# A gated delta-rule attention between two feed-forward layers: key taps ahead of the gates, squares beside the chunks, and the value passes of the next unit spread over four steps

## The chip, the cores and the metric

One Trainium2 chip, one core of it. The metric is the time of one execution on the device in microseconds (us); lower is better. All times below are in us unless ns is written.

## The reference

`x` is 4 sequences of 512 tokens, 512 wide. The output is three residual layers in a row: half a feed-forward layer (2048 wide, its weights spline-interpolated from few control points), a gated delta-rule attention, and half a feed-forward layer again. The change touches the attention alone. Cut to what matters:

```python
q, k, v, z = split(layernorm(x) @ W_qkvz)          # 16 key heads, 32 value heads, 128 wide
q, k, v = silu(causal_conv4(q, k, v))              # four taps along the tokens
q, k = rms_norm(q) / 128, rms_norm(k) / sqrt(128)
for t in range(512):                               # per value head, state 128 x 128
    S = S * exp(g[t])
    delta = (v[t] - k[t] @ S) * beta[t]
    S = S + outer(k[t], delta)
    out[t] = q[t] @ S
y = (silu(z) * rms_norm(out) * norm_w) @ W_out
```

## The kernel before

The attention runs over 64 units, one key head (2 value heads, `R` = 2) of one sequence (512 tokens, 4 chunks of 128, `CH` = 4); four units in a row share a head's weights. The recurrence is done in chunks: per chunk and value head a triangular matrix is inverted, and then a state of 128 x 128 goes from chunk to chunk.

The work is a pipeline with an order written out by hand. Slot `j` of the loop does three things: the delta work of unit `j` (`has_delta`), the preparation of unit `j+1` (`has_prep`: projections, convolution, norms, decays, the matrix to invert), and the output of unit `j-1` (`behind`: scaling, turning and projecting the gated heads). Each engine has its own pass (`pe_pass` L1677, `act_pass` L2005, `dve_pass` L2189, `pool_pass` L2388), runs in order, and waits on counters of the other engines through `wait(engine, name, value)` (L1571 on). The names' first letter tells who counts: s TensorE, a ScalarE, d VectorE, p GpSimd, l loads.

A slot has two parts. The first is steps 2 to 13 (L1882): six levels of the triangular inverse, for the two heads in turn (`g = s % 2`). In each step TensorE makes a product into `psP` (4 matmuls), does what the list `fill[s]` holds, and then the update of the inverse (8 matmuls, L1905 and L1907), for which VectorE must have masked the product (L2336). The product of step s needs ScalarE's copy (`copy_t`, L2090) of the update of step s-2. Then come `residual` (L1912), `fill[14]`, the second residual and `newton` (L1923), `fill[15]`, the second Newton step and the turn of the scaled keys (`turn_kn`, L1784). A residual is followed by VectorE's correction (L2344) that its Newton step needs; ScalarE copies the first inverse out (`inverse_out`, L2140), scales the keys (`scale_k`, L2064, with GpSimd's factor `p_rk`, L2487 to L2491), and then copies the second inverse.

The second part is the loop over the four chunks. TensorE turns the values, subtracts the state's part, makes deltas and outputs and updates the state; between these stand the twelve lists `gap`, with more projections and the decays of the next unit. At the end TensorE projects the next queries (nine passes), ScalarE squares the outputs of both heads (`squares`, L2101, 4 chunks each, an ACTIVATE and a read of the accumulator per chunk), and VectorE multiplies the outputs by the gates (L2378).

What fills the steps:
- Projections of the next unit in passes of 512 columns (`proj_part`, L1702), 12 per unit of keys K, queries Q and two values V0 and V1; gates Z0 and Z1 of this unit in passes of 256 columns (`gate_part`, L1724), 24 each. They use two PSUM banks: K, V0, Z0 the one, Q, V1, Z1 the other. A bank is free when its reader has ended (`bank_free`); for V0 that is the gates' product on VectorE (`silu_z`, L2220, L2223).
- `turn_gated` (L1739, four turns in L1747) of a head that GpSimd has scaled (`scale_gated`, L2438, L2441, behind `out_scale`, L2428, which makes the factor from the squares); ScalarE and VectorE split it in a high and a low half (`gated` L2110, `low` L2243); `out_product` (L1750, six matmuls of 512 columns), of which each of four is added by VectorE (`out_add`, L2248, L2253).
- `turn_k` (L1773, L1781) of the next keys, which ScalarE then squares (`square_k`, L2055, L2061). It overwrites `kn`, which GpSimd's `ks` product (L2469) reads, and so waits for `p_ks`.
- On ScalarE the first tap of a convolution (`tap`, L2015), on VectorE the other three (`conv`, L2204, L2209); the tanh of the silus and gates on ScalarE (`tanh` L2025, `tanh_z` L2038), the silus of K, Q and V1 on GpSimd (`silu`, L2443: L2447 and L2448), in that queue's order: scaling of the heads, V1, K, `kg`, `nllo`, `ks`, Q, the key factor. In the third unit of each head but the last, GpSimd splits half a weight part (L2405 to L2412) between Q and the key factor.
- `qk` (L2225, L2228) on VectorE reads the product of keys and queries from PSUM bank `psM`, into which the next turn goes.

PSUM: `psO[0]` is the upper half of `psT[1]` and `psO[1]` is `psP`, so the outputs of a unit stand where the next unit's level 0 (`level_0`, L1816, head 1 in `fill[2]`) and step products go.

## Time and profile before

| | |
|---|---|
| median of 3 runs | 3610.79 (3608.39 to 3610.88) |
| the profiled execution's own time | 3609.92 |
| its span | 3608.0 |
| TensorE matmul busy | 3391.7, 94% of the span |
| VectorE, ScalarE, GpSimd busy | 2282.5, 2090.2, 2268.8 |
| mean granted TensorE clock | 0.983 of full |

Before the attention stand the splines and the first feed-forward layer (to about 430), behind it the second (from about 3320). A timeline row has start, duration, engine, line, operation, and in brackets the idle time before it with what ended it; an engine's records overlap where it is pipelined, so for TensorE the distance between two starts tells more than the idle time. `PEld` is the weight load of a matmul, SP is the queue of the transfers.

### The profile page before, as it was taken

The page shows a single profiled execution, that of the slowest core. Times are in us where ns is not written, and L with a number is a line of the kernel's source. Part 1 is how long each engine was busy: PE and PEld are TensorE (multiplying, and loading weights), DVE is VectorE, ACT ScalarE, POOL GpSimd, SP SyncE. Part 2 cuts the span into 40 slices and gives each one's busy share as a digit, 9 for nine tenths or more (in the row PEclk, how much of TensorE's full clock was granted, in tenths as well). Part 3 has the DMA queues.
Part 4 walks back from the last instruction along what each step waited for, and adds up shares of the span by engine and source line. Part 5 has one row for each costly group of instructions (what it writes and reads, how often), then busy time and mean ns, then how long its engine had stood idle before and what let it go on. Part 6 is the DMA issues. An engine that isn't in the chain of part 4 may idle for free. (4 is left out here: it accounts for less than half of the span.)

```text
span 3608.0 us, 77463 instructions
## 1 busy us (share of the span) xinstructions
PE 3391.7 (94%) x29092; PEld 2441.0 (68%) x29092; DVE 2282.5 (63%) x4402; ACT 2090.2 (58%) x5699; POOL 2268.8 (63%) x2680
## 2 busy tenths in 40 slices
PE   5997699999999999999999999999999999995998
PEld 3886366666666666666666666666666666663787
DVE  4654566666666666666666666666666666663564
ACT  3443566666666666666666666666666666662343
POOL 2111677777777777777777777777777777772010
PEclk8998899999999999999999999999999999997999
DMA  3524112222222222222222212222222221112421
GB/s 139 180 48 78 49 65 71 76 74 73 78 69 79 75 72 78 68 76 73 76 74 73 79 68 79 68 79 68 79 67 81 66 80 66 59 60 76 141 48 36
DMA packets 217313, 274.46 MB, mean 76 GB/s; under 512 B 91248, under 2 KB 127344, under 8 KB 215792
## 3 DMA queue, kind: packets, MB, share of 16 engines
q1 hardware_dynamic: 207680, 253.60, 22.7%
q0 software_dynamic: 4464, 14.36, 1.1%
q8 instruction: 234, 3.83, 0.5%
q10 hardware_dynamic: 4800, 1.56, 0.3%
q14 instruction: 135, 1.11, 0.1%
HBM read 180.12 MB, written 89.16 MB: 75 GB/s over the span
## 5 line engine op out<-in xcount | busy, mean ns | idle before, releaser
L2099 ACT ACTIVATE at_t<-at_inv 128x512 f16<-128x512 f32 x768 | 460.8, 600 | 434.6 <-PE at_inv L1907 434.4
L2336 DVE TENSOR_TENSOR at_pml<-at_prod,at_cst 128x256 f16<-128x256 f32 x768 | 323.1, 421 | 212.5 <-PE at_prod L1681 201.8
L2483 POOL TENSOR_TENSOR at_gm<-at_cst,at_gates 128x512 fp32r<-128x512 f32 x256 | 268.3, 1069 | 230.3 <-PE at_misc L1681 230.3
L1681 PE MATMUL at_proj<-x_hi,at_w_hi 128*128 128x512 f16 x1024 | 389.3, 380 | 2.8 <-PEq L1267 2.8
L1681 PE MATMUL at_proj<-x_lo,at_w_hi 128*128 128x512 f16 x1024 | 389.8, 381 | 0.0
L1681 PE MATMUL at_proj<-x_hi,at_w_lo 128*128 128x512 f16 x1024 | 389.1, 380 | 0.0
L1905 PEld LDWEIGHTS at_inv<-at_pml,at_t 128*128 128x128 f16 x3072 | 226.4, 97 | 119.0 <-DVE at_pml L2336 81.0
L1681 PE MATMUL at_prod<-at_t,at_nlhi 128*128 128x64 f16 (+1 forms) x3584 | 287.0, 196 | 19.4 <-DVE at_cv_z L2378 15.7
L2209 DVE SCALAR_TENSOR_TENSOR at_cv_v<-at_proj,at_cw,at_cv_v 128x511 f32<-128x511 f32 (+2 forms) x384 | 287.5, 749 | 21.8 <-ACT at_cv_v L2023 8.3
L2253 DVE SCALAR_TENSOR_TENSOR rows<-at_misc,first_tab,rows 128x512 f32<-128x512 f32 x256 | 191.1, 746 | 168.1 <-PE at_misc L1681 168.1
L1905 PE MATMUL at_inv<-at_pml,at_t 128*128 128x64 f16 x3072 | 285.8, 193 | 11.9 <-DVE at_pml L2336 1.1
L1907 PE MATMUL at_inv<-at_t,at_pml 128*128 128x64 f16 x3072 | 283.5, 193 | 0.0
L1681 PE MATMUL at_proj<-at_w_hi,x_hi 128*128 128x256 f16 x1024 | 279.5, 273 | 1.6 <-DVE at_cv_q L2209 0.9
L1681 PE MATMUL at_proj<-at_w_lo,x_hi 128*128 128x256 f16 x1024 | 279.0, 272 | 0.0
L1681 PE MATMUL at_proj<-at_w_hi,x_lo 128*128 128x256 f16 x1024 | 278.9, 272 | 0.0
L1037 PE MATMUL f_ring<-f_x_hi,ffn_w 128*128 128x512 f32 x640 | 247.6, 402 | 3.3 <-DVE f_x_lo L929 2.9
L2165 ACT ACTIVATE at_t<-at_inv,at_gates 128x128 f32<-128x128 f32 x512 | 159.5, 363 | 155.4 <-PE at_inv L1681 155.4
L1681 PEld LDWEIGHTS at_prod<-at_t,at_nlhi 128*128 128x128 f16 x3584 | 190.4, 97 | 82.5 <-issue 45.0
L1907 PEld LDWEIGHTS at_inv<-at_t,at_pml 128*128 128x128 f16 x3072 | 210.3, 98 | 39.2
L1681 PE MATMUL at_misc<-at_wo_hi,at_gt_hi 128*128 128x512 f16 x512 | 198.4, 388 | 22.8 <-DVE at_gt_lo L2246 16.3
L2358 DVE SCALAR_TENSOR_TENSOR at_t<-at_t,at_dcy,at_inv 128x128 f32<-128x128 f32 x256 | 77.6, 345 | 195.9 <-PE at_inv L1681 188.9
L1681 PE MATMUL at_misc<-at_wo_hi,at_gt_lo 128*128 128x512 f16 x512 | 196.1, 383 | 0.0
(323 smaller groups left out, 10124.3 us busy)
## 6 DMA issues: line engine op xcount, KB each, us to landing
rows<-x SPq DMA_DIRECT2D x64, 1024.0 KB, 5.5
x<-rows SPq DMA_DIRECT2D x64, 1024.0 KB, 4.3
at_gb<-decays SPq DMA_DIRECT2D x64, 512.0 KB, 3.7
at_raw_w<-w_qkvz SPq DMA_DIRECT2D x48, 512.0 KB, 7.5
ffn_weights<-ffn_w SPq DMA_DIRECT2D x1, 11776.0 KB, 35.5
ffn_w<-ffn_weights POOLq DMA_DIRECT2D x4, 2688.0 KB, 23.9
at_raw_o<-w_out SPq DMA_DIRECT2D x16, 512.0 KB, 3.5
f_xnext<-x_in SPq DMA_DIRECT2D x4, 1024.0 KB, 5.3
```

The costliest lines, as they stand in the source:

```text
L1037: return nc.tensor.matmul(out, lhsT, rhs, start=start, stop=stop)
L1681: return nc.tensor.matmul(out, lhsT, rhs, start=start, stop=stop)
L1905: nc.tensor.matmul(half_of(ch(psT[g], c), level, 0), ch(t16[:, g, 1], c), half_of(ch(pml[:, level - 1, g], c), level, 0), start=False, sto ...
L1907: last = nc.tensor.matmul(half_of(ch(psT[g], CH + c), level, 1), ch(pml[:, level - 1, g], c), half_of(ch(t16[:, g, 1], c), level, 1), star ...
L2099: own["a_t"].up(A(grown(t16[:, s % R].rearrange("p a t -> p (a t)"), s // R), grown(psT[s % R], s // R), ACT.Copy))
L2165: own["a_d"].up(A(delta[:, h, :], ch(psY, h), ACT.Copy, scale=gcur[:, 2, at + c, h:h + 1]))
L2209: ins = V.scalar_tensor_tensor(out[:, s:S], unit_bank[u][:, 0:S - s], cw[(j + 1) // B % 2][:, u, 3 - s:4 - s], out[:, s:S], ALU.mult, ALU.add)
L2253: own["d_y"].up(V.scalar_tensor_tensor(row, out_bank[:], tab[:, of // B % 2, 7:8], row, ALU.mult, ALU.add))
L2336: own["d_p"].up(V.tensor_tensor(pml[:, level - 1, g].rearrange("p (c b a m) -> p c b a m", c=CH, a=2, m=m)[:, :, :, 0, :], psP[:, 0:S // 2 ...
L2358: ins = V.scalar_tensor_tensor(state[:, h, :], state[:, h, :], dcy[:, j % 2, h, c:c + 1], ch(psU, h), ALU.mult, ALU.add)
L2483: last = G.tensor_tensor(gm[:, k], incl.unsqueeze(1).to_broadcast([P, CH, P]), new_gates[:, g, at:at + CH, h:h + 1].to_broadcast([P, CH, P ...
```

## The change

It moves work between places of the written order, and splits one task.
- `squares` is done per chunk: those of chunks 0 to 2 stand in the chunk loop of ScalarE, behind the deltas (and the second value's tap and first high copy in chunk 2, ahead of the query squares in chunk 1); those of the last chunk at the end, head 1 first. `s_o` counts every chunk and `a_sqo` five per unit (`SQ`). TensorE waits for the squares of chunk c-1 before it writes outputs of chunk c.
- VectorE does all three key taps at the end ahead of the gates (they were one in the chunk loop, one behind the gates, one in step 2), gates head 1 first, and does the first `qk` at the end and the second in step 2 (both were in step 3). TensorE's first product waits for the first gate alone, level 0 and the second head's for both.
- ScalarE: query tap in step 2 (was 4), the gated heads in 2 and 4 (3 and 5), tanh of V1 in 5 (2), of Z0 in 8 (9), key squares in 11 (12). VectorE: `low` in 4 and 6 (5 and 6), first query tap in 5 (6), the fourth `out_add` in 10 (11), the first gates' product in 10 (12).
- TensorE: the gated heads are turned in steps 3 and 5 (4 and 6); Z0 in parts of 4, 6, 4, 6, 4 passes in steps 3 to 7 (5, 5, 5, 2, 7); Z1 in 8 to 13 as 5, 5, 4, 4, 4, 2 (5, 5, 4, 4, 2, 4); the keys turned in 11 (12); V0 in 12 to 15 as 2, 3, 3, 4 passes (14 and 15 as 4, 8).
- GpSimd adds the constant of the norm to `qe` at the end of the preparation (`p_qe`) and not to `sso` behind the squares.

The diff, cut; lines are those of before and after, indentation shortened:

```diff
--- before.py
+++ after.py
@@ -1194,6 +1194,7 @@
 Q_EPS = 64 * D * D * EPS_RMS
+SQ = CH - 1 + R
@@ -1550,11 +1551,11 @@
...
@@ -1819,7 +1820,7 @@
             else:
-                wait(pe, "a_sqo", R * i)
+                wait(pe, "a_sqo", SQ * i)
                 wait(pe, "d_gate", R * i)
@@ -1839,29 +1840,28 @@
         if has_delta:
-            fill[3].append(gates_in(Z0_U, 0, 5))
-            fill[4].append(gates_in(Z0_U, 5, 10))
-            fill[5].append(gates_in(Z0_U, 10, 15))
-        if behind:
-            for h in range(R):
-                fill[4 + 2 * h].append(lambda h=h: turn_gated(h, j - 1))
-        if has_delta:
-            fill[6].append(gates_in(Z0_U, 15, 17))
-            fill[7].append(gates_in(Z0_U, 17, 24))
+            fill[3].append(gates_in(Z0_U, 0, 4))
+            fill[4].append(gates_in(Z0_U, 4, 10))
+            fill[5].append(gates_in(Z0_U, 10, 14))
+            fill[6].append(gates_in(Z0_U, 14, 20))
+            fill[7].append(gates_in(Z0_U, 20, 24))
             fill[8].append(gates_in(Z1_U, 0, 5))
...
             fill[10].append(gates_in(Z1_U, 10, 14))
+            fill[11].append(gates_in(Z1_U, 14, 18))
+            fill[12].append(gates_in(Z1_U, 18, 22))
+            fill[13].append(gates_in(Z1_U, 22, 24))
         if behind:
+            for h in range(R):
+                fill[3 + 2 * h].append(lambda h=h: turn_gated(h, j - 1))
             for c in range(WPROD):
                 fill[7 + c].append(lambda c=c: out_product(c, j - 1))
-        if has_delta:
-            fill[11].append(gates_in(Z1_U, 14, 18))
-            fill[12].append(gates_in(Z1_U, 18, 20))
-            fill[13].append(gates_in(Z1_U, 20, 24))
         if has_prep:
-            fill[12].append(turn_k)
-            fill[14].append(parts(V0_U, 0, 4))
-            fill[15].append(parts(V0_U, 4, 12))
+            fill[11].append(turn_k)
+            fill[12].append(parts(V0_U, 0, 2))
+            fill[13].append(parts(V0_U, 2, 5))
+            fill[14].append(parts(V0_U, 5, 8))
+            fill[15].append(parts(V0_U, 8, 12))
             gap[0].append(parts(V1_U, 0, 3))
@@ -1885,8 +1885,8 @@
                     wait(pe, "a_hi", R * j + g + 1)
-                    wait(pe, "a_sqo", R * j - 1 + g)
-                    wait(pe, "d_gate", R * j)
+                    wait(pe, "a_sqo", SQ * j)
+                    wait(pe, "d_gate", R * j - 1 + g)
                 if s == 2 * R - 1:
@@ -1963,6 +1963,7 @@
                     wait(pe, "p_qg", R * j + R)
+                    wait(pe, "a_sqo", SQ * j + c)
                     for h in range(R):
@@ -1985,9 +1986,8 @@
                     last = mm(ch(psO[h], c), ch(aqk[:, h], c), delta[:, h, :], c == 0, True)
-                if c == CH - 1:
-                    own["s_o"].up(last)
-                else:
+                own["s_o"].up(last)
+                if c < CH - 1:
                     turn_v(c + 1)
@@ -2019,7 +2019,7 @@
             if u == V0_U:
-                wait(act, "s_o", j)
+                wait(act, "s_o", CH * j)
             own["a_tap"].up(A(conv_out(u), unit_bank[u][:], ACT.Copy, scale=cw[(j + 1) // B % 2][:, u, 3:4]))
@@ -2098,13 +2098,15 @@
-        def squares(h):
-            wait(act, "s_o", j + 1)
-            wait(act, "p_fr", j)
-            if h < R - 1:
-                wait(act, "d_gate", R * j + h + 1)
-            for c in range(CH):
-                last = A(osq[:, h, c * P:(c + 1) * P], ch(psO[h], c), ACT.Square, scale=2 * D ** -0.5, accum_out=sso[:, h, c:c + 1])
+        def squares(c, h):
+            if c == 0:
+                wait(act, "p_fr", j)
+            wait(act, "s_o", CH * j + c + 1)
+            return A(osq[:, h, c * P:(c + 1) * P], ch(psO[h], c), ACT.Square, scale=2 * D ** -0.5, accum_out=sso[:, h, c:c + 1])
+
+        def squares_of(c):
+            for h in range(R):
+                last = squares(c, h)
             own["a_sqo"].up(last)
@@ -2115,20 +2117,21 @@
             steps[2].append(lambda: tap(K_U))
-        if has_delta:
-            steps[2].append(lambda: tanh(V1_U, j - 1))
+        if has_prep:
+            steps[2].append(lambda: tap(Q_U))
         if behind:
             for h in range(R):
-                steps[3 + 2 * h].append(lambda h=h: gated(j - 1, h))
+                steps[2 + 2 * h].append(lambda h=h: gated(j - 1, h))
+        if has_delta:
+            steps[5].append(lambda: tanh(V1_U, j - 1))
         if has_prep:
-            steps[4].append(lambda: tap(Q_U))
             steps[6].append(lambda: tanh(K_U))
...
         if has_delta:
-            steps[9].append(lambda: tanh_z(Z0_U))
+            steps[8].append(lambda: tanh_z(Z0_U))
         if has_prep:
-            steps[12].append(square_k)
+            steps[11].append(square_k)
         if has_delta:
@@ -2169,16 +2172,21 @@
                     tanh(V0_U)
+                if c == 2:
+                    tap(V1_U)
+                    high(j + 1, 0)
+            if has_delta and c < CH - 1:
+                squares_of(c)
+            if has_prep:
+                if c == 1:
                     square_q()
                 if c == 2:
-                    tap(V1_U)
-                    for g in range(R):
-                        high(j + 1, g)
+                    high(j + 1, 1)
         if has_prep:
...
             for h in reversed(range(R)):
-                squares(h)
+                own["a_sqo"].up(squares(CH - 1, h))
         if has_prep:
@@ -2222,9 +2230,9 @@
-        def qk(h):
-            wait(dve, "s_kq", j + 1)
-            wait(dve, "a_sqo", R * j)
+        def qk(i, h):
+            wait(dve, "s_kq", i + 1)
+            wait(dve, "a_sqo", SQ * i)
             own["d_aqk"].up(V.scalar_tensor_tensor(aqk[:, h, :], psM[:], -1.0, e2[:, h, :], ALU.mult, ALU.mult))
@@ -2305,26 +2313,21 @@
         steps = {s: [] for s in range(STEPS)}
-        if has_prep and has_delta:
-            steps[2].append(lambda: conv(K_U, (3,)))
         if has_delta:
-            for h in range(R):
-                steps[3].append(lambda h=h: qk(h))
+            steps[2].append(lambda: qk(j, 1))
         if has_prep and not has_delta:
...
         if behind:
-            steps[5].append(lambda: low(0, j - 1))
+            for h in range(R):
+                steps[4 + 2 * h].append(lambda h=h: low(h, j - 1))
         if has_prep:
-            steps[6].append(lambda: conv(Q_U, (1,)))
-        if behind:
-            steps[6].append(lambda: low(1, j - 1))
-        if has_prep:
+            steps[5].append(lambda: conv(Q_U, (1,)))
             steps[7].append(lambda: conv(Q_U, (2, 3)))
...
             for c in range(WPROD):
-                steps[7 + c + c // (WPROD - 1)].append(lambda c=c: out_add(c, j - 1))
+                steps[7 + c].append(lambda c=c: out_add(c, j - 1))
         if has_delta:
-            steps[12].append(lambda: silu_z(Z0_U))
+            steps[10].append(lambda: silu_z(Z0_U))
         for s in range(R, STEPS):
@@ -2369,15 +2372,15 @@
                     conv(K_U, (1,), j + 1)
+        if has_prep and j + 2 < UNITS:
+            conv(K_U, (2, 3), j + 1)
         if has_delta:
-            for h in range(R):
-                if h == 0:
-                    wait(dve, "s_o", j + 1)
-                else:
-                    wait(dve, "a_sqo", R * j + h)
+            for h in reversed(range(R)):
+                wait(dve, "s_o", CH * (j + 1))
+                wait(dve, "a_sqo", SQ * (j + 1) - h)
                 own["d_gate"].up(V.tensor_tensor(gated_of(h), psO[h].rearrange("p (c v) -> p c v", c=CH), gated_of(h), ALU.mult))
-        if has_prep and j + 2 < UNITS:
-            conv(K_U, (2,), j + 1)
+        if has_prep:
+            qk(j + 1, 0)
         if ends:
@@ -2427,17 +2430,16 @@
-            wait(pool, "a_sqo", R * (of + 1))
-            wait(pool, "a_sq", of)
+            wait(pool, "a_sqo", SQ * (of + 1))
+            wait(pool, "p_qe", of + 1)
             flat = sso[:].rearrange("p h c -> p (h c)")
             chain(G.tensor_tensor(sso[:], sso[:], qe[:, of % 2, :].unsqueeze(1).to_broadcast([P, R, CH]), ALU.add))
-            chain(G.tensor_scalar(flat, flat, Q_EPS * EPS_RMS, None, ALU.add))
             own["p_fr"].up(G.tensor_tensor(fr[:].rearrange("p h c -> p (h c)"), flat, half[:, 0:R * CH], ALU.pow))
...
-            wait(pool, "d_gate", R * of + h + 1)
+            wait(pool, "d_gate", R * (of + 1) - h)
             own["p_gt"].up(G.tensor_tensor(gated_of(h), gated_of(h), fr[:, h, :].unsqueeze(2).to_broadcast([P, CH, D]), ALU.mult))
@@ -2448,7 +2450,7 @@
         if has_delta:
-            wait(pool, "s_o", j)
+            wait(pool, "s_o", CH * j)
             wait(pool, "a_knT", j)
@@ -2510,6 +2512,8 @@
                 own["p_t0"].up(G.affine_select(right, right, [[0, CH], [-2, P // 2]], ALU.not_equal, 1.0, base=-1, channel_multiplier=1))
+            wait(pool, "a_sq", j + 1)
+            own["p_qe"].up(G.tensor_scalar(qe[:, nxt, :], qe[:, nxt, :], Q_EPS * EPS_RMS, None, ALU.add))
             if j == 0:
```

## Rows read from the trace of the kernel before

**Rows 1.** the page: span, and busy time of the engines
```profile
span 3608.0 us, 77463 instructions
...
PE 3391.7 (94%) x29092; PEld 2441.0 (68%) x29092; DVE 2282.5 (63%) x4402; ACT 2090.2 (58%) x5699; POOL 2268.8 (63%) x2680
```

**Rows 2.** windows, columns: stretch, its length, busy us and instructions of each engine, clock, DMA
```profile
480.00:3200.00 2720.00, 2653.74 (x25127) 1883.43 (x25128) 1806.64 (x3529) 1727.25 (x4970) 2038.87 (x2335) 1.00 0.23 73
3294.00:3318.00 24.00, 13.16 (x32) 4.37 (x32) 4.39 (x6) 1.19 (x2) 3.60 (x3) 0.50 0.03 12
```

**Rows 3.** waits of TensorE's weight loads, 1000 to 3000 us: total, times, longest
```profile
PEld at_inv L1905 <- DVE at_pml L2336: 54.3, 178, 0.4
```

**Rows 4.** timeline of TensorE, one unit: start, length, engine, line, operation, count, idle before
```profile
1509.53 0.66 PE L1747 MATMUL at_misc<-at_cst,at_cv_z 128*128 128x128 f32 x4 [0.33 <-POOL at_cv_z L2441]
...
1515.78 0.27 PE L1681 MATMUL at_proj<-at_w_hi,x_hi 128*128 128x256 f16 x1
...
1523.32 0.20 PE L1905 MATMUL at_inv<-at_pml,at_t 128*128 128x64 f16 x1
...
1525.80 0.22 PE L1681 MATMUL at_prod<-at_t,at_nlhi 128*128 128x128 f16 x1
...
1527.29 0.22 PE L1681 MATMUL at_prod<-at_t,at_nlhi 128*128 128x128 f16 x1
...
1529.90 0.61 PE L1787 MATMUL at_misc<-at_cst,at_kn 128*128 128x128 f32 x4
```

**Rows 5.** timeline of ScalarE, end of the unit: first and last of 16 square instructions
```profile
1548.42 0.28 ACT L2107 ACTIVATE at_aqk<-at_prod 128x128 f32<-128x128 f32 x1 [0.16 <-PE at_prod L1681]
...
1550.34 0.25 ACT L2107 ACTIVATION_READ_ACCUMULATOR at_aqk<-at_inv 128x1 f32 x1
```

**Rows 6.** timeline of VectorE, end of the unit
```profile
1546.86 0.75 DVE L2209 SCALAR_TENSOR_TENSOR at_cv_k<-at_proj,at_cw,at_cv_k 128x511 f32<-128x511 f32 x1 [0.61 <-ACT at_cv_k L2023]
...
1549.59 0.69 DVE L2378 TENSOR_TENSOR at_cv_z<-at_prod,at_cv_z 128x512 f32<-128x512 f32 x1 [0.41 <-ACT at_aqk L2107]
```

**Rows 7.** timeline of TensorE, end of the unit
```profile
1549.94 0.38 PE L1681 MATMUL at_proj<-x_hi,at_w_lo 128*128 128x512 f16 x1
...
1550.54 0.28 PE L1681 MATMUL at_prod<-at_t,at_nlhi 128*128 128x64 f16 x4 [0.22 <-DVE at_cv_z L2378]
1550.69 0.38 PE L1681 MATMUL at_inv<-at_pm,at_cst 128*128 128x512 f16 x1
```

**Rows 8.** timeline of GpSimd, the same unit
```profile
1506.07 0.20 POOL L2433 TENSOR_TENSOR at_sso<-at_sso,at_qe 128x8 f32<-128x8 f32 x1 [2.88 <-ACT at_aqk L2107]
...
1506.36 0.25 POOL L2434 TENSOR_SCALAR at_sso<-at_sso 128x8 f32<-128x8 f32 x1
...
1508.43 2.04 POOL L2441 TENSOR_TENSOR at_cv_z<-at_cv_z,at_fr 128x512 f32<-128x512 f32 x2
...
1514.15 1.27 POOL L2447 TENSOR_TENSOR at_th<-at_th,at_cv_k 128x512 f32<-128x512 f32 x1 [1.08 <-ACT at_th L2036]
...
1520.87 1.61 POOL L2469 TENSOR_TENSOR at_ks<-at_kn,at_gates 128x384 f32<-128x384 f32 x2
```

**Rows 9.** timeline of VectorE, steps 11 and 12
```profile
1523.17 0.74 DVE L2253 SCALAR_TENSOR_TENSOR rows<-at_misc,first_tab,rows 128x512 f32<-128x512 f32 x1
...
1524.22 0.68 DVE L2223 SCALAR_TENSOR_TENSOR at_cv_z<-at_th,at_proj 128x512 f32<-128x512 f32 x1
```

**Rows 10.** timeline of ScalarE, behind step 15
```profile
1528.65 1.13 ACT L2068 ACTIVATE at_kn<-at_misc,at_scale 128x128 f32<-128x128 f32 x4
```

**Rows 11.** timelines of GpSimd, ScalarE and TensorE, third unit of a head
```profile
1618.19 0.20 POOL L2491 TENSOR_TENSOR at_scale<-at_rr,at_cst 128x4 f32<-128x4 f32 x1
...
1618.42 1.14 ACT L2068 ACTIVATE at_kn<-at_misc,at_scale 128x128 f32<-128x128 f32 x4
...
1619.62 0.66 PE L1787 MATMUL at_misc<-at_cst,at_kn 128*128 128x128 f32 x4
```

**Rows 12.** timeline of TensorE, end of the last unit
```profile
3296.73 1.12 PE L1747 MATMUL at_misc<-at_cst,at_cv_z 128*128 128x128 f32 x4 [5.75 <-POOL at_cv_z L2441]
```

More of the change, by code:

```diff
@@ L1552, in attn_phase @@
                  "d_conv", "d_silu", "d_z", "d_nl", "d_aqk", "d_p", "d_e", "d_s", "d_gate", "d_lo", "d_y", "d_max_w", "d_max_o", "d_tab", "d_scaled", "d_scaled_o", "d_link",
[L1553 removed]
+                 "p_w", "p_wo", "p_z", "p_gt", "p_silu", "p_gm", "p_ex", "p_diag", "p_t0", "p_lo", "p_dcy", "p_kg", "p_qg", "p_ks", "p_rk", "p_fr", "p_qe", "p_link"]
         sems = {n: sem(n) for n in names}
[L1557 removed]
+        AHEAD = {"s_proj": 4, "s_qtr": 1, "s_ktr": 2, "s_dg": R,  "a_tap": 4, "a_th": 4, "a_ssk": 1, "a_sq": 1, "a_kn": 1, "a_knT": 1, "a_ex": R,
                  "d_conv": 4, "d_silu": 1, "p_silu": 3, "p_gm": R, "p_ex": R, "l_x": -32, "l_kq": -16, "l_v": -16, "l_z": -16, "l_wo": -16, "l_taps": -48, "p_w": -2, "p_z": -1, "p_rk": 1}
```

2 lines of the change are left out of this document (removed).

## The prediction

> **What bounds the kernel now.** I read the page first: of the span of 3608.0 us TensorE is busy 94%, the next engine 63% [rows 1]. The table of windows puts 2720 us of it, the 61 middle turns of the attention loop, at full granted clock, 2.4 GHz [rows 2]. So the attention is a TensorE stream with holes, and what an edit can win is a hole. The list of TensorE's waits names many small ones, the largest sum being the updates of a step behind VectorE's masked product, 54.3 in 2000 us [rows 3]. The timelines of one unit, which repeats every 44.75 us, then give each hole its place. I quote times of one unit; its first step product started at 1505.79, and that of the next unit starts at 1550.54. Matmul records overlap, so a hole is read from start to start: a pass of 256 columns follows another in 0.11, one of 512 in 0.22, and so the first gated head's turn at 1509.53 stands behind a hole of 0.50, of which its row shows 0.33 [rows 4].
>
> **The tail of a unit.** ScalarE squares the outputs in 16 instructions, from 1548.42 to 1550.59, 0.25 per chunk and head [rows 5]. The change leaves two of the eight, so the last ends at about 1549.05; the other six go into the chunk loop, a pair of 0.5 behind each chunk's outputs. There ScalarE waits for TensorE, so I cost them at nothing; without that cover each pair costs 0.5. The wait of chunk c+1 for these squares is over 0.2 to 0.6 before TensorE gets there. VectorE now runs all three key taps before the gates. They start at 1546.86, 0.75 each and one behind the other's end, so the gates, 0.61 apart, end at about 1549.78 and 1550.39, where the second ended at 1550.28 before [rows 6]. The first product no longer waits for the second gate and goes when the pass that starts at 1549.94 lets it, 1550.16; but level 0 of head 1, right behind it, does wait, and comes about 0.17 after the gate's end. That is 1550.55, where it stood 0.15 behind the product of 1550.54, at 1550.69: gain 0.15 [rows 7].
>
> **Steps 2 to 7.** GpSimd's scaling began with the squares' end: sum 1506.07, constant 1506.36, power, scaling 1508.43 [rows 8]. Squares 1.54 earlier and the constant (0.33 to the next start) taken out bring the scaling to 1506.55 and its first head to 1507.6. The turn, moved to step 3, is due at 1507.72: its hole of 0.50 closes. With fills of four and six passes, and a turn beside each four, the holes behind the mask's products close too, but ScalarE's longer queue (query taps and first gated head ahead of the copy of step 3) opens two of 0.15 at steps 5 and 7. Summed, Z1's first pass goes at 1514.39 and not at 1515.78 [rows 4]: 1.39 ahead. Steps 8 to 10 are as before and keep it.
>
> **Steps 10 to 13.** VectorE's fourth output sum (0.75) moves ahead of the mask of step 11, and the first gates' product (0.68) with it. In the old clock the sum was ready to start about 1522.49 but ran at 1523.17, then the gates at 1524.22 [rows 9]. Now: sum at 1521.10, gates 1521.76, mask of step 11 not before 1522.37 to 1522.79, updates of step 11 at 1522.82. They stood at 1523.32 [rows 4]; with the key turn (0.45) ahead of them I expect some 0.6 of holes in this step, and only 0.5 left of the 1.39. Steps 12 and 13 have fills of 0.87, longer than the 0.68 that a product's way through VectorE takes, so their holes close. They hold five of the values' twelve passes, 1.08 of work. The residual of head 0 starts at about 1525.5, against 1525.80 [rows 4].
>
> **Steps 14 and 15 give no more.** From there the time is a chain, not a stream: residual 1525.80, its correction by VectorE, second residual 1527.29 (1.49 later), Newton step, copy, scaled keys 1528.65 to 1529.78 on ScalarE [rows 4, 10], turn of the keys 1529.90: 4.10, of which 4.07 is chain. Before, 2.59 of value passes filled it. Now 1.51 do, so the 1.08 that left comes back as holes, about 0.4 before the second residual and 0.8 before the turn. The unit gains what the residual's start gains: **0.3 us**. A unit's later part, to 1550.16, is TensorE's own work, and moves with it.
>
> **The price on GpSimd.** The tanh of the second values goes from ScalarE's step 2 to step 5, where it ends at about 1512.55. GpSimd, in order, sits idle from 1508.6, and starts that silu at 1512.62, not behind the scaling's 2.04 at 1510.43. The key silu behind it then starts at 1515.22, where it started at 1514.15 after a wait [rows 8]: everything behind it is **1.07 later** while TensorE is earlier. In ordinary units the keys' factor would come at 1527.76, and ScalarE wants it at 1528.36: cover 0.6. The keys' products for the state end at 1523.57, not 1522.48, and the key squares want them at 1523.74: cover 0.2. But in the third unit of each head GpSimd splits weights between the query silu and this factor. There it is the bound already: factor ready at 1618.39, scaled keys from 1618.42, turn 1619.62 [rows 11]. All of that gets 1.07 later; whatever TensorE has won before is lost in front of the turn.
>
> **Sum.** The factor's delay falls in 15 units (heads 0 to 14), the gain in the 47 others of the 62 that have a unit behind and one ahead. The last unit gains 1.7 at its end, where TensorE waits 5.75 for the scaling [rows 12], and 0.7 in its steps. So -47 x 0.3 + 15 x 1.07 - 2.4 = -14.1 + 16.1 - 2.4 = -0.4. The profiled execution's 3609.92 (span 3608.0) becomes 3609.5; it lies 0.87 under the median of the runs, 3610.79, so I predict **3610**. Edits at nothing: the constant added at GpSimd's unit end (0.25, idle there until the squares' end), the key squares in step 11 (ScalarE has finished the copy), the first z tanh in step 8 (it needs the key silu, 1515.22 and two operations of 1.3 on, and ends at 1518.5, before the copy of step 9 at 1519.0), the half high copy behind the squares in chunk 2. Within 0.2%, 7 us, a measurement can't tell a change.
>
> **Unknown prices.** The gain of an ordinary unit is at least nothing (the chain of 4.07 alone doesn't grow) and at most 0.5, where the copy of step 12, behind the key squares, stops it. The loss of a third unit is 0.8 if the tanh comes sooner by a step's copy, 1.3 if TensorE is later at step 5. A wait on two semaphores costs 0.06 to 0.26 (the latter from the gate's end, 1550.28, to the first product, 1550.54 [rows 6, 7]); I took 0.17 for level 0.
>
> **Rivals.** *Faster*: step 11 goes through sooner, so ordinary units gain 0.5, and the third units lose 0.8: -23.5 + 12 - 2.4 = -14, 3597. For it: the early steps win 1.39. Against: VectorE's queue is in order. *Slower*: VectorE's two products ahead of the mask of step 11 cost more. If its updates start after 1523.1, the residual isn't earlier, ordinary units gain nothing, and the split units stand alone: +16.1 - 2.4 = +14, 3624. For it: three dependent waits in a row in one step, each of which I took at its shortest. Against: 0.3 of room. *The clock*: in the third units TensorE would stand idle for 2.5 in front of the turn. After the last unit's outputs it idled 5.75, and the clock stood at 0.50, 1.2 GHz, behind that [rows 2, 12]; in the loop, with holes of at most 0.5, it never fell. Were it to fall in 15 units and stay low for the 5 us of one chunk, that is +75, 3685. The Trainium skill (TensorE: Matmul & The Clock Gate, Part 1) says that the throttled state is the default and that activity releases it, which speaks against this change. The last unit agrees; no row shows a pause of 2.5.
>
> **How the numbers follow.** The forecast 0.40, with its own range 3603 to 3617; the faster rival 0.33, the slower 0.22, the clock 0.05. So faster 0.33, same 0.40, slower 0.27. The range 3591 to 3627 takes in the first three with 0.2 per third unit and 0.1 per ordinary one, and leaves out the clock.
>
> **What would show it.** Ordinary units about 44.45 apart; units behind a third one 1 longer than now. Turn of the gated head without a wait; Z1's first pass 1.4 earlier from the unit's start; the updates of step 11 waiting for VectorE; holes of about 0.4 and 0.8 ahead of the second residual and of the keys' turn; in third units scaled keys waiting for GpSimd and a hole near 2.5. I am wrong if the holes ahead of the turn stay under 0.3, if third units aren't longer, or if the copies of steps 3 and 5 hold TensorE by more than 0.3.

## The result: 0.54% slower, and the profile after

The changed kernel takes 3630.36 us (median of 4, 3628.58 to 3632.58), the kernel before 3610.84 beside it: ratio 1.0054 [1.0039, 1.0069]. The prediction, 3610 with a range of 3591 to 3627, was wrong. It gave 0.27 to slower, and 0.05 to the mechanism that did it.

The page of the changed kernel: span, engine totals, one group (busy and mean ns, then idle before it with what ended it).

```profile
span 3628.8 us, 77659 instructions
PE 3373.7 (93%) x29092; PEld 2482.1 (68%) x29092; DVE 2273.6 (63%) x4402; ACT 2100.8 (58%) x5699; POOL 2263.5 (62%) x2680
L2449 POOL TENSOR_TENSOR at_th<-at_th,at_cv_v 128x512 f32<-128x512 f32 x64 | 81.4, 1272 | 257.0 <-ACT at_th L2036 257.0
```

The engines do the work of [rows 1]; GpSimd now idles 257 us in front of the second values' silu. The table of windows (columns as in [rows 2]):

```profile
480.00:3200.00 2720.00, 2613.89 (x24991) 1904.96 (x24990) 1788.46 (x3508) 1727.15 (x4935) 2019.94 (x2319) 0.99 0.22 72
1630.00:1634.00 4.00, 3.56 (x18) 3.06 (x19) 0.23 (x2) 2.52 (x8) 2.91 (x4) 0.68 0.04 8
3297.20:3303.90 6.70, 5.99 (x26) 5.43 (x26) 0.49 (x2) 1.63 (x7) 0.00 (x0) 0.50 0.00 1
```

The granted clock of the loop, 1.00 in [rows 2], is 0.99. The second row is one of the places: 4 us behind the pause of a third unit, part at 1.2 and part at 2.4 GHz. The third lies in the last unit.

**Where the 20.8 us of span are.** I measured each unit from start to start, by ScalarE's first copy of the inverse in it (`copy_t`). Ordinary units went from 44.76 to 44.39, 0.37 less. Third units went from 45.00 to 45.98 in two of the 15 (those of heads 0 and 8) and to 47.44 to 47.50 in the other 13. The granted clock is at half for one short stretch in exactly those 13, just behind the pause, and otherwise only in the first unit, which went from 42.12 to 44.51, and the last. So the loop: -47 x 0.37 + 2 x 0.98 + 13 x 2.46 + 2.4 = +19.0; measured from the first unit's start to the last's, +19.3. Of the 2.46 a third unit loses 0.98 to GpSimd's later factor and 1.48 to the fall of the clock. The work ahead of the loop (+1.0) and from the last unit on (+0.5) makes up the rest.

An ordinary unit, on TensorE. I count from its level 0, 1560.74 here and 1505.94 before (a unit ahead of the one in [rows 7]):

```profile
1562.67 0.60 PE L1748 MATMUL at_misc<-at_cst,at_cv_z 128*128 128x128 f32 x4
...
1569.21 0.28 PE L1682 MATMUL at_proj<-at_w_hi,x_hi 128*128 128x256 f16 x1
...
1577.75 0.20 PE L1905 MATMUL at_inv<-at_pml,at_t 128*128 128x64 f16 x1 [0.21 <-DVE at_pml L2339]
...
1581.91 0.22 PE L1682 MATMUL at_prod<-at_t,at_nlhi 128*128 128x128 f16 x1 [0.23 <-DVE at_pm L2347]
...
1584.46 0.66 PE L1788 MATMUL at_misc<-at_cst,at_kn 128*128 128x128 f32 x4 [0.63 <-ACT at_kn L2068]
```

The gated head is turned without a wait. Z1's first pass comes 8.47 behind level 0, where by [rows 4] it was 9.84: 1.37 earlier. The updates of step 11 are 0.37 earlier (17.01 against 17.38), the second residual 0.18, the keys' turn 0.24, now behind a wait of 0.63. The other 0.13 of the unit is at its end, in front of level 0.

The third unit of a head, unit 26 counted from nought, on ScalarE, GpSimd and TensorE, where [rows 11] have it before:

```profile
1611.18 0.63 ACT L2036 ACTIVATE at_th<-at_cv_v 128x512 f32<-128x512 f32 x1
1611.89 1.27 POOL L2449 TENSOR_TENSOR at_th<-at_th,at_cv_v 128x512 f32<-128x512 f32 x1 [3.94 <-ACT at_th L2036]
...
1629.01 0.20 POOL L2493 TENSOR_TENSOR at_scale<-at_rr,at_cst 128x4 f32<-128x4 f32 x1
1629.24 1.14 ACT L2068 ACTIVATE at_kn<-at_misc,at_scale 128x128 f32<-128x128 f32 x4 [1.48 <-POOL at_scale L2493]
...
1627.83 0.39 PE L1682 MATMUL at_inv<-at_t,at_pm 128*128 128x128 f16 x4
1630.44 0.66 PE L1788 MATMUL at_misc<-at_cst,at_kn 128*128 128x128 f32 x4 [2.22 <-ACT at_kn L2068]
...
1632.13 1.06 PE L1682 MATMUL at_inv<-at_t,at_sq 128*128 128x128 f32 x4
1632.98 1.92 PE L1682 MATMUL at_inv<-at_knT 128*128 128x128 f32 x8
```

Read from the top, it is the chain that was predicted: tanh late, silu late, factor late, scaled keys late, and TensorE's pause of 2.39 (1627.83 plus its four passes at 0.055, to 1630.44). The last two rows are what was not: eight matmuls take 1.92 where they take 1.10 at full clock. From the first slow one some 15 matmuls follow one another 0.10 later each, 1.48 in all: 47.46 against 45.98. The list of TensorE's waits, 1000 to 3000 us (total, times, longest), puts it first:

```profile
PE at_misc L1788 <- ACT at_kn L2068: 45.3, 44, 2.2
```

### The profile page after: what moved, and what is told of

It reads as the page before. It is cut to its first block and busy times, and to the rows that moved or that the text cites. A ratio compares the mean times of both kernels' runs of the same rounds, so it can differ in the third digit from the quotient of the medians.

```text
span 3628.8 us, 77659 instructions
## 1 busy us (share of the span) xinstructions
PE 3373.7 (93%) x29092; PEld 2482.1 (68%) x29092; DVE 2273.6 (63%) x4402; ACT 2100.8 (58%) x5699; POOL 2263.5 (62%) x2680
## 5 line engine op out<-in xcount | busy, mean ns | idle before, releaser
L2449 POOL TENSOR_TENSOR at_th<-at_th,at_cv_v 128x512 f32<-128x512 f32 x64 | 81.4, 1272 | 257.0 <-ACT at_th L2036 257.0
```

The costliest lines, as they stand in the source:

```text
L2449: chain(G.tensor_tensor(th[:, u % 2, :], th[:, u % 2, :], x, ALU.mult))
```

## The experiments

They ran beside the kernel before, which took 3611 to 3614 there. "Holes" are measured start to start, as in the prediction. Lengths of units and counts of falls (third units with the granted clock at half) are those of one execution per kernel, the profiled one; the times are medians of 2 to 10 executions.

### One: is it the late tanh?

e1, the change with the tanh two steps earlier:

```diff
-                    steps[5].append(lambda: tanh(V1_U, j - 1))
+                    steps[3].append(lambda: tanh(V1_U, j - 1))
```

> The changed kernel with the tanh of the second values in ScalarE's step 3 instead of 5, nothing else. Theory A (the late silu on GpSimd makes third units wait, the wait lets the clock fall): the silu starts at about 10.1 in the unit's clock and the key silu at 13.7, not 15.2, so the key factor in third units comes 1.5 earlier, the hole before the keys' turn is near 1.0 and the clock stays at 1.00; third units 44.9 to 45.2 apart instead of 47.46, ordinary ones 44.4 as now; in all 3593 to 3599. Theory B (the spread value passes thin out TensorE's work, and that lets the clock fall): the clock still falls in third units; they are 46 to 46.5, in all 3610 or more.

Measured: 3587.91, ratio 0.9923 [0.9908, 0.9937]. Ordinary units stay at 44.40; third units are 44.40 as well, without a fall, and the first is 42.78. I had expected 44.9 to 45.2 for the third units and 3593 to 3599 in all, too long both times. Its third unit, on GpSimd and TensorE:

```profile
1591.79 1.27 POOL L2449 TENSOR_TENSOR at_th<-at_th,at_cv_v 128x512 f32<-128x512 f32 x1 [1.54 <-ACT at_th L2036]
...
1611.16 0.66 PE L1788 MATMUL at_misc<-at_cst,at_kn 128*128 128x128 f32 x4 [0.64 <-ACT at_kn L2068]
...
1613.06 1.10 PE L1682 MATMUL at_inv<-at_knT 128*128 128x128 f32 x8
```

GpSimd waits 1.54 in place of 3.94, the pause is 0.80 as in every other unit, and the eight matmuls take 1.10. One number of the change cost 1.3% of the kernel, 47 us by the ratios: 24 in the third units without their falls (15 x 1.58), 19 for the 13 falls, 2 in the first unit. Without it the change is 0.8% faster than before.

### Two: the same tanh put late in the kernel before

```diff
-                    steps[2].append(lambda: tanh(V1_U, j - 1))
+                    steps[5].append(lambda: tanh(V1_U, j - 1))
```

> The kernel before with one edit: tanh of the second values in ScalarE's step 5 instead of 2. Theory A: the silu on GpSimd starts behind that tanh, some 2 later, the key silu 1.4 to 2.0 later; ordinary units keep 44.76 if the factor still comes in time, third units go from 45.0 to 46.4 or 47; the hole before the keys' turn is 1.6 to 2.2, perhaps too short for the clock to fall: 3610.8 + 15 x 1.4 to 2.0 = 3632 to 3641 with no fall. Theory B: no fall, whatever the hole. If the clock falls here too, the spread has no part in it.

Measured: 3657.66, ratio 1.0117 [1.0102, 1.0132]. Third units 46.73, a pause of 1.53, no fall. I missed the ordinary units: 45.15, not 44.76. All of the 0.39 is at the first output product of step 7 (hole 0.83, was 0.46). In the old order the second gated head is copied on ScalarE in step 5 too, and the tanh stands ahead of what VectorE and then TensorE wait for. So a place that is free in the changed order costs 47 x 0.39 = 18 us in the old one.

### Three: the values' passes not spread

e2, the change with the values' passes as before:

```diff
-                    fill[12].append(parts(V0_U, 0, 2))
-                    fill[13].append(parts(V0_U, 2, 5))
-                    fill[14].append(parts(V0_U, 5, 8))
-                    fill[15].append(parts(V0_U, 8, 12))
+                    fill[14].append(parts(V0_U, 0, 4))
+                    fill[15].append(parts(V0_U, 4, 12))
```

> The changed kernel with the values' passes back as 4 in step 14 and 8 in step 15, none in 12 and 13. Theory A: in third units 0.86 more work stands ahead of the hole, but the factor comes when it came, so the hole shrinks from 2.4 to 1.3 or 1.5 and the clock stays; third units 45.9 apart, 3611 +- 4 in all if ordinary units keep their 44.4. In ordinary units holes of 0.25 and 0.45 open in steps 12 and 13 and those of 0.39 and 0.79 before the keys' turn close to 0.2 in sum; they come out at 44.2 to 44.5. Theory B: the same without falls. Theory C (the spread is what pays): ordinary units go back to 44.7.

Measured: 3609.51, ratio 0.9988 [0.9979, 0.9997]. Ordinary units 44.37, the same as with the spread: the holes only move. They are 0.25, 0.46, 0.29 and 0.18 from step 12 to the second residual, where the spread has 0.39 and 0.80 behind that; both sums are 1.2. Third units 45.97, a pause of 1.58, no fall:

```profile
1625.52 0.65 PE L1788 MATMUL at_misc<-at_cst,at_kn 128*128 128x128 f32 x4 [1.41 <-ACT at_kn L2066]
...
1627.41 1.10 PE L1682 MATMUL at_inv<-at_knT 128*128 128x128 f32 x8
```

45.97 is also what the two third units without a fall show in the changed kernel, whose pause is 2.39. So the pause's length, for itself, costs nothing here: the factor's chain sets the unit. Only what follows the pause differs: 13 x 1.48, 19 us.

### Four: a pause filled with work nobody needs

e5, the change with eight needless passes of 512 columns in step 15 of the third units, ahead of the turn. It computes nothing that is used:

```diff
                     fill[15].append(parts(V0_U, 8, 12))
+                    if has_delta and j % B == B - 2 and j // B + 1 < NK:
+                        def idle_work():
+                            for k in range(8):
+                                mm(psT[0][:, S:2 * S], ident16, x_hi[:, k % HB, 0:S])
+                        fill[15].append(idle_work)
```

> The changed kernel with 8 needless matmuls of 512 columns (1.73 us of work into an unused part of PSUM, behind the last value passes of step 15) in the 15 third units alone. Theory A (the clock falls because TensorE idles for 2.4 us there): they fit in the hole, the factor comes when it came, and the clock stays at 1.00; third units go from 47.46 to 45.98, the length of the two in which it did not fall; in all 3630.4 - 13 x 1.48 = 3611. Theory A' (the fall is only a coincidence and the 1.48 is another wait): third units stay at 47.4, 3630, or get longer.

Measured: 3614.33, ratio 0.9999 [0.9989, 1.0009]: 16 us less than the change (20 by the ratios), with 120 matmuls more. Third units 46.0, pause 0.67, no fall:

```profile
1622.80 0.66 PE L1788 MATMUL at_misc<-at_cst,at_kn 128*128 128x128 f32 x4 [0.50 <-ACT at_kn L2073]
1624.15 0.70 PE L1682 MATMUL at_inv<-at_t,at_sq 128*128 128x128 f32 x4
1624.69 1.10 PE L1682 MATMUL at_inv<-at_knT 128*128 128x128 f32 x8
```

The turn waits for the same factor, the matmuls behind it run at 0.70 and 1.10, not 1.06 and 1.92. Since nothing behind the factor differs in order or work, this shows the clock as the cause of the 1.48. The changed kernel's own two third units without a fall, at 45.98 with the same pause, agree.

g3 and g4 do it with three passes and with one:

> Kernel: the changed kernel with three needless passes of 512 columns (results in a part of a bank that the next product starts anew) behind the values' last passes in step 15 of the third units. Pause in front of the keys' turn 2.39 - 0.66 = 1.73. Theory (a pause of 1.55 leaves the clock alone and one of 2.39 doesn't; the nearer length decides): no fall, third units 45.98, the time as with eight such passes, 3612 to 3616. Rival (a pause above 1.6 is enough): falls in most of 15, third units 47.4, 3633.

> Kernel: as the one with three needless passes, with one: pause 2.39 - 0.22 = 2.17. In the changed kernel 13 of 15 pauses of 2.39 had a fall behind them. Theory (2.39 lies at the edge, since two of fifteen went without): falls in fewer units, 0 to 5, third units 45.98 but for those: 3614 to 3622. Rival (2.39 is far above the edge and the two without a fall are something else): 13 or so falls, 3632 to 3634.

With three (pause 1.73): 3609.80, ratio 0.9991 [0.9981, 1.0000], no fall. With one (pause 2.17): 3616.51, ratio 1.0014 [1.0003, 1.0025], but its ten runs spread from 3610.50 to 3626.69, 16 us, where those of each other kernel lie within 1 to 10 us. The profiled one, 3625.73, has 8 falls in the loop's third units, at 47.44 to 47.54, beside 7 at 45.98. My "0 to 5" was too low for that run; the median, 9 us below it, suggests that most runs have fewer.

### Five: how long must the pause be?

g2, the kernel before with the tanh in step 6:

```diff
-                    steps[2].append(lambda: tanh(V1_U, j - 1))
+                    steps[6].append(lambda: tanh(V1_U, j - 1))
```

> Kernel: the kernel before, with the tanh of V1 in ScalarE's step 6 (there were 3661 to 3654 with it in step 5, a hole of 1.53 in the third units and no fall). The passes of V0 stay at 4 and 8 in steps 14 and 15. Both theories: the silu of V1 starts near 14.5 in the unit's time, 1.4 later than with step 5; the hole in front of the keys' turn grows to about 2.9 in third units and to 1 to 1.5 in ordinary ones; ordinary units 46.0 to 46.7. Theory (the pause by itself makes the clock fall): the granted clock is at half for a short stretch right behind it in most of the 15 third units, which are then 1.5 longer than the hole explains; 47 x 1.6 + 15 x (3.1 + 1.5) = +144, 3755 or so. Rival (the fall needs the changed kernel's order, in which the values' passes are spread over four steps ahead of the pause): no fall in the loop, 15 x 3.1, about 3733.

Measured: 3702.28, ratio 1.0243 [1.0228, 1.0258]. Ordinary units 45.47, less than I expected, since the hole in front of their turn is 0.67. Third units have the longest pause of all, 3.10, and 12 of 15 have no fall (47.90), three have one (49.2 to 49.45). One without:

```profile
1659.53 0.66 PE L1787 MATMUL at_misc<-at_cst,at_kn 128*128 128x128 f32 x4 [2.93 <-ACT at_kn L2068]
1660.89 0.70 PE L1681 MATMUL at_inv<-at_t,at_sq 128*128 128x128 f32 x4
1661.43 1.10 PE L1681 MATMUL at_inv<-at_knT 128*128 128x128 f32 x8
```

Neither theory held: a pause by itself can do it, but 3.10 did it in 3 of 15 and 2.39 in 13. (The profiled execution took 3694.10, the three others 3700.55 to 3704.08. If falls are all of the difference, that is 4 to 7 more at 1.48 each, so 3 need not be this kernel's usual count. Experiment six shows why it can vary.)

### Six: same pause, heads further apart

Three kernels keep the pauses and the order around them, and lengthen each head's first unit by needless passes in step 15. h1 is the one of experiment five with eight passes, h2 and h3 are the change with eight and with twelve:

```diff
+                    if has_delta and j % B == 0:
+                        def idle_work():
+                            for k in range(8):
+                                mm(psT[0][:, S:2 * S], ident16, x_hi[:, k % HB, 0:S])
+                        fill[15].append(idle_work)
```

> Kernel: the kernel before with the tanh of V1 in step 6 (pauses of 3.10 in the third units, behind which the clock fell in 3 of 15; four units 184.3 apart), and besides it eight needless passes of 512 columns in step 15 of each head's first unit. They fill its hole of 0.67 in front of the keys' turn and make that unit about 1.1 longer, so the heads lie 185.4 apart; the pause and what surrounds it stay. Theory (where the pause falls in time decides whether it costs a fall, since every head repeats the same distance): another count, 6 to 12 of 15. Rival (the pause's surroundings decide: with the values' passes late, as before the change, the clock holds): again 1 to 5 of 15. Time by the theory 3702 + 16 x 1.1 + 6 x 1.5 = 3729; by the rival 3720.

> Kernel: the changed kernel (pauses of 2.39, a fall behind 13 of 15) and besides it eight needless passes in step 15 of each head's first unit, which is then about 1.0 longer (its hole of 0.80 is filled first). Theory (where the pause falls in time): another count than 13, 4 to 10, the third units without a fall at 45.98. Rival (surroundings): 13 to 15 again. Time by the theory 3630 + 16 x 1.0 - 6 x 1.48 = 3637; by the rival 3646.

> Kernel: as the one before it with twelve needless passes in place of eight; the first units are about 1.85 longer than in the changed kernel. Theory (where the pause falls in time): a third count, and with the heads at this distance it may be as low as 0 to 4 of 15, since a head without a fall is followed by another at the same place. Rival (surroundings): 13 to 15. Time by the theory 3630 + 16 x 1.85 - 11 x 1.48 = 3643; by the rival 3660.

| kernel | pause | first unit of a head | falls of 15, profiled | profiled | other executions | median |
|---|---|---|---|---|---|---|
| g2 | 3.10 | 45.47 | 3 | 3694.10 | 3700.55 to 3704.08 | 3702.28 |
| h1 | 3.10 | 46.48 | 9 | 3718.80 | 3720.39 | 3719.60 |
| the change | 2.39 | 44.39 | 13 | 3630.64 | 3628.58 to 3632.58 | 3630.36 |
| h2 | 2.39 | 45.27 | 8 | 3633.71 | 3639.31, 3641.48 | 3639.31 |
| h3 | 2.39 | 46.12 | 0 | 3642.05 | 3639.92 | 3640.99 |

The counts were another each time, as the theory had it. For the profiled executions the times add up: h1 is g2 with 16 x 1.01 and 6 x 1.48 more, 3719.1 against the 3718.8 measured. But a count is that of one execution. By the medians h3 has 17.1 less than its longer units alone would give (16 x 1.73), some 12 falls fewer than the change, and h2 has 5.1 less, three or four fewer. Between g2 and h1 the medians show less than one fall more. The pair that carries the argument is the change and h3. The window of h2, then that of h3, and a third unit of h3:

```profile
480.00:3200.00 2720.00, 2623.21 (x25062) 1906.36 (x25061) 1785.60 (x3504) 1728.56 (x4931) 2014.28 (x2314) 0.99 0.22 72
```

```profile
480.00:3200.00 2720.00, 2623.38 (x25087) 1900.90 (x25086) 1785.27 (x3502) 1724.79 (x4931) 2016.55 (x2316) 1.00 0.22 72
```

```profile
1635.60 0.39 PE L1682 MATMUL at_inv<-at_t,at_pm 128*128 128x128 f16 x4
1638.21 0.66 PE L1788 MATMUL at_misc<-at_cst,at_kn 128*128 128x128 f32 x4 [2.22 <-ACT at_kn L2073]
1639.56 0.70 PE L1682 MATMUL at_inv<-at_t,at_sq 128*128 128x128 f32 x4
1640.10 1.10 PE L1682 MATMUL at_inv<-at_knT 128*128 128x128 f32 x8
```

h3 has the very pause of the changed kernel, 2.22 before the same matmul, and goes on at full clock in all 15. Between h2 and h3 lie four passes, two units ahead of each pause. So when the pause comes decides, beside its length. The Trainium skill (TensorE: Matmul & The Clock Gate, Part 1) says that what the gate watches runs free of the kernel's own start; these runs agree, and the traces show the place itself.

**Where each pause begins.** In every record of the granted clock here, the changes lie on one even grid of times, to within 0.01 us, from the kernel's start to its end. Let the place of a pause be its start as a share of the grid's step, from 0 at a grid time to 1 at the next. The third units' pauses, sorted by place:

| pause | kernels | with a fall | without a fall |
|---|---|---|---|
| 3.10 | g2, h1 | 12, at 0.68 through 1 to 0.23 | 18, at 0.45 to 0.68 |
| 2.39 | the change, h2, h3 | 21, at 0.92 through 1 to 0.36 | 24, at 0.39 to 0.84 |
| 2.17 | g4 | 8, at 0.96 through 1 to 0.36 | 7, at 0.39 to 0.93 |
| 1.73 | g3 | 0 | 15, at 0.09 to 0.20 and 0.61 to 0.72 |
| 1.58 | e2 | 0 | 15, at 0.04 to 0.25 and 0.58 to 0.73 |
| 1.53 | e4 | 0 | 15, at 0.08 to 0.97 |

No place has both for one length (at 3.10 they meet at 0.68, 0.677 without and 0.680 with), and a longer pause has a wider range of places with a fall. All 15 places of h3 lie at 0.46 to 0.59. Twelve of g2's lie at 0.59 to 0.67, close below the edge at 0.68: an execution whose pauses begin a little later on the grid would get more falls. That fits its three slower executions but is not shown, since they have no trace. The places also explain the 13: in the changed kernel a head with a fall is 180.6 us long, and its place moves back by 0.10 or less from head to head. At head 8 it is at 0.84, outside the range. That head has no fall and is 1.5 shorter, and the next pause begins at 0.32, inside again.

### Seven: what the rest of the change is worth

All on e1, one edit after another. f1 puts the first gates' product (`silu_z`) from VectorE's step 10 to step 11, behind the mask; f2 adds the key squares in ScalarE's step 12 and the values' passes as 1, 2, 4, 5; g1 adds the keys' tanh in step 5. f3 is e1 with the third key tap behind the gates, f4 is g1 with that tap.

```diff
-                    steps[10].append(lambda: silu_z(Z0_U))
+                    steps[11].append(lambda: silu_z(Z0_U))
```

> e1 (tanh of the second values in step 3) and VectorE's first gates' product in step 11, behind that step's mask, not ahead of it. Theory A (VectorE's order holds the updates of step 11, and the residual behind them starts the chain that ends the unit): the hole of 0.37 ahead of those updates goes, the residual starts 0.3 earlier, units are 44.1 apart instead of 44.40; ratio to before 0.987. Theory B (the unit is held further on, by ScalarE's key squares ahead of its copy of step 12): the hole goes but units stay at 44.3 to 44.4; ratio 0.992 as e1.

f1: 3565.25, ratio 0.9864 [0.9850, 0.9879]. Ordinary 44.00: the hole of 0.37 in front of the updates of step 11 is gone.

```diff
-                    steps[11].append(square_k)
+                    steps[12].append(square_k)
...
-                    fill[12].append(parts(V0_U, 0, 2))
-                    fill[13].append(parts(V0_U, 2, 5))
-                    fill[14].append(parts(V0_U, 5, 8))
-                    fill[15].append(parts(V0_U, 8, 12))
+                    fill[12].append(parts(V0_U, 0, 1))
+                    fill[13].append(parts(V0_U, 1, 3))
+                    fill[14].append(parts(V0_U, 3, 7))
+                    fill[15].append(parts(V0_U, 7, 12))
```

> f1 with the key squares back in ScalarE's step 12 and the values' passes as 1, 2, 4, 5 in steps 12 to 15 instead of 2, 3, 3, 4. Theory A (steps 12 and 13 need fills of 0.65 to cover VectorE, what is above only delays the residual; from the residual on it is a chain of 4.07): the residual starts 0.7 earlier than in the changed kernel; ordinary units 43.7 apart, third units 44.2 to 44.3, since GpSimd's factor comes no earlier there; ratio 0.982 to 0.984. Rival (the passes spread are worth their place): no gain over f1, 0.987.

f2: 3549.24, ratio 0.9818 [0.9801, 0.9834]. Ordinary 43.65, third 44.21: the pause there is 1.14 against 0.58, set by the factor.

```diff
-                    steps[6].append(lambda: tanh(K_U))
+                    steps[5].append(lambda: tanh(K_U))
```

> Kernel: that of the run with the key squares in step 12 and the values' passes as 1, 2, 4 and 5 (3549.24), and besides it the tanh of the keys in ScalarE's step 5, not 6; the third key tap stays ahead of the gates, as in the change. Theory (GpSimd's queue sets the third units, and nothing else does): the key silu starts earlier, the keys' factor is ready about 0.6 sooner, third units come from 44.21 to the ordinary 43.65, no hole over 0.7 in front of the keys' turn, no fall of the clock in the loop: 15 x 0.56 = 8.4 less, 3541, ratio 0.979 to 0.980. Rival (the tanh lengthens the way of ScalarE's copy of step 5 or 6): ordinary units get 0.1 to 0.2 longer, +5 to +9, and the time stays at 3546 to 3551.

g1: 3538.49, ratio 0.9795 [0.9781, 0.9810], the fastest here and 2.6% under the change by the ratios. All units 43.65, third ones included:

```profile
1588.22 0.66 PE L1788 MATMUL at_misc<-at_cst,at_kn 128*128 128x128 f32 x4 [0.41 <-ACT at_kn L2068]
```

The tap:

```diff
-                    conv(K_U, (2, 3), j + 1)
+                    conv(K_U, (2,), j + 1)
...
+                if has_prep and j + 2 < UNITS:
+                    conv(K_U, (3,), j + 1)
                 if has_prep:
                     qk(j + 1, 0)
```

> e1 with the third key tap behind the gates on VectorE, ahead of the first product of queries and keys. Theory A (the three taps ahead of the gates are why level 0 of the second head still waits 0.24): the gates end 0.25 earlier, the hole of 0.24 goes, and nothing waits for the tap or for that product; units 44.2 apart; ratio 0.988. Rival: what comes 0.2 later then (first mask of the unit, second product) takes it back: 44.4, ratio 0.992.

> f2 and f3 together, and the tanh of the keys in ScalarE's step 5 instead of 6, so that GpSimd's key silu follows the one of the second values at once. Theory A: the gains add: ordinary units 43.5 apart, third units 43.7 to 44.1; ratio 0.978 to 0.980, clock at 1.00 throughout the loop. Rival: the chains meet (the factor, or the key squares) and f4 is no more than 0.2 per unit under f2.

f3: 3596.20, ratio 0.9952 [0.9937, 0.9967]: 44.55, 0.15 more than e1. The hole in front of level 0 shrinks from 0.24 to 0.07, and one of 0.41 opens at the updates of step 2, whose mask now stands behind the tap on VectorE; I had expected a gain. f4: 3549.22, ratio 0.9821 [0.9806, 0.9835], all units 43.82, no better than f2, so the gains did not add. It differs from g1 by the tap alone: taps first is right, by 0.17 a unit.

## Why the prediction was wrong, point by point

- **What bounds the kernel**: right. Whatever closed a hole in an ordinary unit came back in the time.
- **The tail**: right. VectorE's three taps are one block and the gates follow, and level 0 starts 0.15 behind their end; 0.17 was taken.

```profile
1601.47 2.31 DVE L2217 SCALAR_TENSOR_TENSOR at_cv_k<-at_proj,at_cw,at_cv_k 128x511 f32<-128x511 f32 x3 [0.61 <-ACT at_cv_k L2023]
1603.70 0.68 DVE L2381 TENSOR_TENSOR at_cv_z<-at_prod,at_cv_z 128x512 f32<-128x512 f32 x1
1604.30 0.68 DVE L2381 TENSOR_TENSOR at_cv_z<-at_inv,at_cv_z 128x512 f32<-128x512 f32 x1
```

- **Steps 2 to 13**: right. Z1's first pass 1.39 ahead was predicted, 1.37 came; 0.5 was to be left behind step 11, and 0.37 was, the holes there being 0.31 and 0.37 where I took 0.6 together. VectorE's mask runs behind its two products as described:

```profile
1576.01 0.75 DVE L2261 SCALAR_TENSOR_TENSOR rows<-at_misc,first_tab,rows 128x512 f32<-128x512 f32 x1 [1.23 <-PE at_misc L1682]
1576.68 0.68 DVE L2231 SCALAR_TENSOR_TENSOR at_cv_z<-at_th,at_proj 128x512 f32<-128x512 f32 x1
1577.27 0.42 DVE L2339 TENSOR_TENSOR at_pml<-at_prod,at_cst 128x256 f16<-128x256 f32 x1
```

- **Steps 14 and 15 as a chain**: right. The hole in front of the keys' turn is 0.80, predicted 0.8; in front of the second residual 0.39, predicted 0.4. e2 shows the consequence, which I had stated: the spread buys nothing. The ordinary unit gains 0.37, predicted 0.3.
- **The price on GpSimd**: right. 0.98 in third units without a fall, predicted 1.07; a pause of 2.39, predicted 2.5.
- **The last unit**: half right. The wait for the scaling fell from 5.75 [rows 12] to 3.84, 1.9 (predicted 1.7).

```profile
3317.37 0.91 PE L1748 MATMUL at_misc<-at_cst,at_cv_z 128*128 128x128 f32 x4 [3.84 <-POOL at_cv_z L2443]
```

  But 6.7 us of its chunks ran at half clock (the third window above), and its last outputs came 2.2 later from the unit's start than before, which took it back.
- **The sum and the chances**: here a step failed, the clock's term, which the sum and the range left out. By the mechanisms that I summed the kernel comes to 3609.5; e2, g3 and e5, which have them and no fall in the third units, have ratios of 0.9988, 0.9991 and 0.9999, 3606.5 to 3610.5. The rest is the rival "the clock". I had its mechanism and the unit that it strikes, and gave it 0.05, with the words that no row shows a pause of 2.5. But no row excluded it either: the holes that I had read in the loop ended at 0.5, and the next pause that I had read was 5.75, with the low clock behind it. The trace of the kernel before has one between, in the loop's first unit, ahead of the stretch of [rows 2]: a pause of 1.69, at full clock, that ends with this row:

```profile
450.24 0.23 PE L1681 MATMUL at_prod<-at_t,at_nlhi 128*128 128x128 f16 x1 [1.36 <-ACT at_t L2099]
```

  So 2.5 stood in the open stretch between 1.69 and 5.75, and a chance of a third would have been nearer to what the rows supported. And its price was too high by more than three: I let the clock stay low for the 5 us of a chunk, 5 each, where a fall cost 1.48. 13 x 1.48 is 19, not 75. At 1.5 each and a chance of a third, the range would have had to reach 3632.
- **The first unit**, which I had left out of the sum, has a fall too, behind a pause of 2.56 (450.34 to 452.91), and lost 2.4. Not all of it is the fall: e1, with a pause of 2.57 there and no fall, lost 0.7.
- The Trainium skill says in TensorE: Matmul & The Clock Gate, Part 1, that throttled is the default and activity releases it. The traces agree: behind 13 pauses of 2.39 the granted clock stood at half, and after some 15 matmuls without a pause at full again.

What stays open: how short a pause can have a fall behind it. The shortest seen with one in the third units is 2.17. The kernels at 1.53, 1.58 and 1.73 do not owe their full clock to when their pauses came: many of these began at places where 2.17 and 2.39 always had a fall. So in this stream the limit lies between 1.73 and 2.17. It is no limit for thinner work: in the last unit, where nothing is prepared, the clock fell at 3297.2 with no pause above 1.04 in the 6 us before it, but five of 0.30 to 1.04 one behind the other.

## What to carry to other kernels

A task moved to a later place in one engine's queue is to be followed through the queue behind it into the rarest kind of iteration, since a tight one may exist there only. When a change concentrates waiting into one pause on TensorE of 2 us or more, where no row shows such a pause at full clock, count with a chance of a clock fall and about 1.5 us for each. Here holes of the same sum spread out avoided it (a pause of 1.58), and so did needless matmuls in the pause (down to 1.73). The same pause can cost nothing or a fall by where it begins, so a count from one execution is not the kernel's. And when a kernel's runs spread more than usual, look for falls that come in some runs only.

## What was not expected of the hardware

- A fall of the granted clock cost 1.48 us in a stream that is otherwise dense: f32 matmuls of 128 columns followed each other in 0.21 and not 0.11.
- The same pause of 2.39 had a fall behind 13, 8 or 0 of 15, by the distance between heads. By the place on the grid of the clock's changes the pauses of 1.53 to 3.10 divide without an exception.
- With a pause of 2.17 the same kernel took 3610.50 to 3626.69 over ten runs. Profiled, 8 of 15 pauses had a fall; a difference of 11 falls, at 1.48 each, would be the whole spread.
- 120 matmuls that nobody needs made a kernel 16 us faster.
